# A Mamba-style decoder on one core: softplus through a PSUM bank, relu on ScalarE, and a later turn of the second half's projection

## The reference, cut to what matters

```python
ssm = x @ W_x.T                                  # 1024 -> 32 + 16 + 16
ts, Bm, Cm = (rms(ssm[..., :R]), rms(ssm[..., R:R + N]), rms(ssm[..., R + N:]))
dt = jax.nn.softplus(ts @ W_dt.T + b_dt)         # one step size for each channel and time
A = -jnp.exp(A_log)
def step(state, inp):
    dA = jnp.exp(dt_t[..., None] * A)
    state = state * dA + (dt_t * u_t)[..., None] * B_t[:, None, :]
    y = jnp.einsum('bdn,bn->bd', state, C_t)
```

## Time and profile before

| | |
|---|---|
| median of 3 runs | 1512.21 us (1509.62 to 1515.13) |
| the profiled execution | 1510.68 us, its span 1508.8 us |
| mean granted TensorE clock | 0.953 |
| the loop's scans | first starts at 132.45 us; rounds 32, 64 and 96 start at 248.90, 365.33 and 483.70 us |
| a loop round without softplus work | 2.68 us |

### The profile page before, as it was taken

How to read it: one execution, slowest core, us unless ns; L and a number is a source line. 1 busy time by engine, 2 the same in 40 slices (tenths; PEclk the granted TensorE clock), 3 DMA queues, 4 the chain that set the end, 5 groups by cost and what they waited for, 6 DMA issues and landing times.

```text
span 1508.8 us, 18407 instructions
## 1 busy us (share of the span) xinstructions
PE 1332.5 (88%) x6448; PEld 959.5 (64%) x6448; DVE 967.0 (64%) x1687; ACT 741.5 (49%) x1447; POOL 670.0 (44%) x488
## 2 busy tenths in 40 slices
PE   7996767768768988988999999799999899999996
PEld 5884556556557665444455555478888788778774
DVE  6745978978878987688654443554444456455566
ACT  4446779779778884122122222254444344434431
POOL 3228769769769871121461111263333244333321
PEclk9998889879979999999999999699999999999999
DMA  4121000013000005100200000132212122111110
GB/s 142 43 113 57 1 0 1 1 56 112 1 1 1 1 1 163 70 15 1 90 2 27 15 1 15 42 107 68 66 68 70 56 84 71 63 63 60 53 57 28
DMA packets 29546, 71.20 MB, mean 47 GB/s; under 512 B 3376, under 2 KB 3632, under 8 KB 27536
## 3 DMA queue, kind: packets, MB, share of 16 engines
q1 hardware_dynamic: 29456, 70.04, 13.9%
HBM read 67.86 MB, written 2.16 MB: 46 GB/s over the span
## 4 chain that ended last, share of the span: by engine, by line
PE 66%; DVE 15%; ACT 9%; issue 6%; POOL 2%; DMA 1%; SPq 0%; DVEq 0%; POOLq 0%; ACTq 0%
PE psum L453 9%; PE psum L455 9%; PE psum L454 9%; ACT arena L889 6%; DVE arena L1550 5%; PE psum L524 5%; PE psum L837 4%; PE psum L707 3%; PE psum L864 3%; PE psum L701 3%; PE psum L538 3%; ACT psum L889 2%; PE psum L618 2%; PE psum L549 2%; PE psum L856 2%
## 5 line engine op out<-in xcount | busy, mean ns | idle before, releaser
L1550 DVE TENSOR_TENSOR_SCAN arena<-psum,arena 128x512 f32<-128x512 f32 x256 | 298.0, 1208 | 74.2 <-ACT psum L889 74.1
L1296 POOL TENSOR_TENSOR arena<-arena 128x1024 f32<-128x1024 f32 x128 | 302.1, 2381 | 88.0 <-DVE arena L1550 86.7
L1229 POOL TENSOR_TENSOR w_split<-arena,w_split 128x512 fp32r<-128x512 f32 x128 | 168.1, 1334 | 311.9 <-ACT w_split L889 311.8
L524 PE MATMUL psum<-prm,arena 128*128 128x128 f32 x1024 | 179.3, 308 | 106.2 <-DVE arena L1550 66.6
L524 PEld LDWEIGHTS psum<-prm,arena 128*128 128x128 f32 x1024 | 127.0, 155 | 177.4 <-DVE arena L1550 128.2
L889 ACT ACTIVATE arena<-psum,ssmn 128x256 f32<-128x256 f32 x480 | 191.7, 497 | 51.5 <-PE psum L524 50.5
L889 ACT ACTIVATE arena<-psum 128x512 f32<-128x512 f32 (+2 forms) x178 | 100.8, 577 | 232.8 <-PE psum L707 53.6
L889 ACT ACTIVATE psum<-arena,amat 128x508 f32<-128x508 f32 x256 | 172.2, 725 | 30.9 <-DVE arena L1550 30.7
L889 ACT ACTIVATE arena<-arena 128x512 f32<-128x512 f32 x112 | 69.5, 633 | 228.0 <-DVE arena L1765 223.7
L538 PE MATMUL psum<-prm,arena 128*128 128x128 f32 x1024 | 148.5, 293 | 0.1
L889 ACT ACTIVATE arena<-psum,prm 128x512 f32<-128x512 f32 (+1 forms) x130 | 89.4, 700 | 117.5 <-PE psum L701 54.3
(11 more groups left out here) (221 smaller groups left out, 2475.7 us busy)
## 6 DMA issues: line engine op xcount, KB each, us to landing
arena<-wq SPq DMA_DIRECT2D x64, 256.0 KB, 2.5
arena<-wo SPq DMA_DIRECT2D x64, 256.0 KB, 2.9
arena<-bc_scratch SPq DMA_DIRECT2D x8, 1024.0 KB, 4.8
arena<-win SPq DMA_DIRECT2D x16, 256.0 KB, 2.6
arena<-xT SPq DMA_DIRECT2D x8, 256.0 KB, 6.1
x_tok<-xtok SPq DMA_DIRECT2D x1, 2048.0 KB, 8.1
arena<-wout SPq DMA_DIRECT2D x8, 256.0 KB, 5.5
arena<-ctxtok SPq DMA_DIRECT2D x1, 2048.0 KB, 8.0
```

Source lines behind the costliest of these rows:

```text
L524: last = nc.tensor.transpose(hT[:, c, b % 2, e, :], hst[:, (2 * k + e) % 4, b * L:(b + 1) * L], ident)
L1229: gp.tensor_tensor(out_, whole, hi.bitcast(F32), ALU.subtract).then_inc(done, 1)
L1296: gp.tensor_tensor(bu[:, i % 4, :, :], dtu[:, (2 * j + e) % 4, :].unsqueeze(1).to_broadcast([P, NG, HT]), Brep[:, q * NG:(q + 1) * NG, :], ...
L1550: v.tensor_tensor_scan(hst[:, i % 4, :], dA[:, i % 3, :], bu[:, (k // NG * 2 + e) % 4, k % NG, :], 0.0, ALU.mult, ALU.add).then_inc(S.scan ...
```

## The change

Four things are edited. (1) `dt_bank` gives the first four blocks banks of their own (6, 7, 5, 3); `dt_proj` no longer waits for a relu, and from block 4 on waits until the previous block's correction is done (`dt_w`), since the bank is now in use until then. (2) e is written into the block's PSUM bank in place of the tile dt in SBUF, and both instructions of `one_plus` read it there. (3) Relu is computed on ScalarE, right ahead of |v|, and is gone from VectorE. (4) `ssm_turn(1)` moves from ahead of `in_proj(31)` to round 22 of the loop and its evacuation `turned_ssm(1)` to round 23; on GpSimd `ssm_rstd(1)` moves ahead of `step_size(1)` and `step_in(1)`.

```diff
+        def dt_bank(M):
+            return bank[(6, 7, 5, 3)[M] if M < GP else 5]
...
             def dt_proj(M):
                 h, m = M // MD, M % MD
-                if M % MD in (0, GP):
-                    pe.wait_ge(S.ssmT_sb, (1 if M == 0 else 2))
+                if m == 0:
+                    pe.wait_ge(S.ssmT_sb, h + 1)
                 if M >= GP:
-                    pe.wait_ge(S.dt_relu, M)
-                elif M >= 2:
-                    pe.wait_ge(S.dt_relu, M - 1)
-                mm(bank[6 + M % 2 if M < GP else 5][:, :], wdt_sb[:, m * P:(m + 1) * P], ssmT[0:RK, h, :],
+                    pe.wait_ge(S.dt_w, M)
+                mm(dt_bank(M)[:, :], wdt_sb[:, m * P:(m + 1) * P], ssmT[0:RK, h, :],
...
-            in_proj(BACK + 4)
-            in_proj(BACK + 5)
-            ssm_turn(1)
-            in_proj(BACK + 6)
-            pe.wait_ge(S.dt_relu, GP)
+            for n in range(BACK + 4, len(UNITS)):
+                in_proj(n)
+            pe.wait_ge(S.dt_w, GP)
...
+                if k == 22:
+                    pe.wait_ge(S.dt_w, 2 * GP)
+                    ssm_turn(1)
...
             def abs_dt(M):
                 act.wait_ge(S.dt_proj, M + 1)
-                av(dt[:, M % MD, :], bank[6 + M % 2 if M < GP else 5][:, :], ACT.Abs,
-                   bias=pc("bdt")[:, M % MD:M % MD + 1]).then_inc(S.dt_abs, 1)
+                bias = pc("bdt")[:, M % MD:M % MD + 1]
+                av(sp_r[:, M % GP, :], dt_bank(M)[:, :], ACT.Relu, bias=bias).then_inc(S.dt_relu, 1)
+                av(dt[:, M % MD, :], dt_bank(M)[:, :], ACT.Abs, bias=bias).then_inc(S.dt_abs, 1)
 
             def exp_dt(M):
                 act.wait_ge(S.dt_abs, M + 1)
-                av(dt[:, M % MD, :], dt[:, M % MD, :], ACT.Exp, scale=-1.0).then_inc(S.dt_exp, 1)
+                av(dt_bank(M)[:, :], dt[:, M % MD, :], ACT.Exp, scale=-1.0).then_inc(S.dt_exp, 1)
...
-            in_out(BACK + 4)
-            in_out(BACK + 5)
-            turned_ssm(1)
-            in_out(BACK + 6)
+            for n in range(BACK + 4, len(UNITS)):
+                in_out(n)
...
+                    if k == 23:
+                        turned_ssm(1)
...
-            for M in range(2):
-                step_size(M)
-                step_in(M)
+            step_size(0)
+            step_in(0)
             ssm_rstd(1)
+            step_size(1)
+            step_in(1)
...
-            def relu_dt(M):
...
             def one_plus(M):
                 dve.wait_ge(S.dt_exp, M + 1)
-                v.tensor_scalar(sp_w[:, M % GP, :], dt[:, M % MD, :], 1.0, None, ALU.add).then_inc(S.dt_w0, 1)
+                v.tensor_scalar(sp_w[:, M % GP, :], dt_bank(M)[:, :], 1.0, None, ALU.add).then_inc(S.dt_w0, 1)
                 dve.wait_ge(S.dt_w0, M + 1)
-                v.scalar_tensor_tensor(out=dt[:, M % MD, :], in0=sp_w[:, M % GP, :], scalar=1.0, in1=dt[:, M % MD, :],
+                v.scalar_tensor_tensor(out=dt[:, M % MD, :], in0=sp_w[:, M % GP, :], scalar=1.0, in1=dt_bank(M)[:, :],
                                        op0=ALU.subtract, op1=ALU.subtract).then_inc(S.dt_w, 1)
...
-                    if r in (4, 8, 12, 16):
-                        relu_dt(M + r // 4 - 1)
```

More of the change, by code:

```diff
@@ L1519, in ssm_normed @@
                         ins.then_inc(S.ssm_norm, 1)
-            def relu_dt(M):
-                dve.wait_ge(S.dt_abs, M + 1)
-                v.tensor_scalar(sp_r[:, M % GP, :], bank[6 + M % 2 if M < GP else 5][:, :],
-                                pc("bdt")[:, M % MD:M % MD + 1], 0.0, ALU.add, ALU.max).then_inc(S.dt_relu, 1)
             def one_plus(M):
                 dve.wait_ge(S.dt_exp, M + 1)
-                v.tensor_scalar(sp_w[:, M % GP, :], dt[:, M % MD, :], 1.0, None, ALU.add).then_inc(S.dt_w0, 1)
+                v.tensor_scalar(sp_w[:, M % GP, :], dt_bank(M)[:, :], 1.0, None, ALU.add).then_inc(S.dt_w0, 1)
                 dve.wait_ge(S.dt_w0, M + 1)
-                v.scalar_tensor_tensor(out=dt[:, M % MD, :], in0=sp_w[:, M % GP, :], scalar=1.0, in1=dt[:, M % MD, :],
+                v.scalar_tensor_tensor(out=dt[:, M % MD, :], in0=sp_w[:, M % GP, :], scalar=1.0, in1=dt_bank(M)[:, :],
                                        op0=ALU.subtract, op1=ALU.subtract).then_inc(S.dt_w, 1)
@@ L1559, in _ @@
             for M in range(GP):
-                relu_dt(M)
-            for M in range(GP):
                 one_plus(M)
```

## The result

The kernel after took 1473.93 us in the median of four runs (1470.52 to 1478.39) against 1510.91 of the kernel before: a ratio of 0.9752, with a 95% interval of 0.9718 to 0.9786. The forecast was 1480 with a range of 1466 to 1493. Measured a second time (E9), on another chip, the same kernel took 1477.15 us (ratio 0.9777, 0.9753 to 0.9802). The profiled execution took 1475.01 us; its span is 35.6 us shorter than that of before.

What follows compares the result with a forecast made beforehand. ScalarE was taken to bound plain rounds at 2.68 us, idling 4.02 us per `one_plus`. Loop 26.5 plus start 6.5 less 0.7 for the turn gave 32.3 us off 1510.68, 1478.4; forecast 1480, range 1466 to 1493.

Steps and rivals of the forecast that it cites:

- The bound and the stall: Scan loop: ScalarE bounds plain rounds at 2.68 us and idles 4.02 us (2.85 plus 1.17) for each `one_plus`.
- Why `one_plus` was slow: VectorE in the loop: its two instructions spread to medians of 1695 and 2716 ns; those with a PSUM operand don't spread.
- `one_plus` at 1.43: VectorE in the loop: with operands in PSUM, 0.73 plus 0.70 makes 1.43 us in place of 4.37.
- Idle time of ScalarE for each `one_plus`: Scan loop: falls from 4.02 to 1.05 us, saving 3.0 us for each of nine `one_plus`.
- Relu 0.57 on ScalarE: Ahead of the next decays: relu adds 0.57 us to the path for each of twelve blocks.
- e into PSUM, 0.09 more: ScalarE's exp in the loop: writing PSUM instead of SBUF costs 0.09 us more each, between 0 and 0.15.
- A cycle at 13.3 us, 2.34 less: Four loop rounds: 3.0 - 0.57 - 0.09 = 2.34 us saved, from 15.68 to 13.3; nine such cycles give 21.1.
- stretches at 1.2 GHz, which I had as a gain that might come: Warmer-TensorE rival in the loop: shorter stalls may keep 2.4 GHz, 9 us more at most, 1471 to 1477; chance 0.10.
- The start, 6.5: Ahead of the loop: without the turn the first scan starts 6.5 us earlier, limited by GpSimd's tile; bounds 4 and 7.6.
- The wait of `dt_proj`: TensorE in round 5: waiting for the correction costs 0, at most the matmul's own 0.6 us.
- GpSimd's rival: Scan loop: GpSimd, busy 12.89 us a cycle, takes over the wait; 12 us lost, 1492; chance 0.13.
- The slow `one_plus` as a rival: Scan loop: any SBUF operand holds VectorE up while GpSimd runs; loop loses 9.5 us, time 1517; chance 0.04.

Runs made afterwards that it cites:

- E9: The kernel after, unchanged, timed again beside the kernel before on another chip: 1477.15 us, ratio 0.9777.
- E1: The kernel after with e written in place into the SBUF tile dt again and read there by `one_plus`, relu still on ScalarE: 1517.09 us, ratio 1.0044.
- E3: The kernel after with e of blocks 4 to 15 in an SBUF tile of its own in place of the PSUM bank: 1516.99 us, ratio 1.0043.
- E8: The kernel before with only the second half's turn moved to round 22, its evacuation to 23 and GpSimd's power up by two: 1504.47 us, ratio 0.9965.
- E2: The kernel after with the second half's turn, its evacuation and GpSimd's power back ahead of the loop: 1478.51 us, ratio 0.9792.

## Why the prediction was right, step by step

- *The bound and the stall*: right. E1 and E3 bring the stall back (2.41 and 1.17 us, 3.6 in all for 4.02), and E8, which has the slow `one_plus` of before, keeps the cycles of before (15.67 to 16.24 us).
- *Why `one_plus` was slow*: the prediction gave no mechanism, only that instructions with a PSUM operand don't spread. The end of GpSimd's tile as what releases it was found in the traces afterwards (E3).
- *`one_plus` at 1.43*: 1.30 from start to start. L1529 was expected at 0.73 like L1523 and took 0.66; L1531 0.69 for 0.70.
- *Idle time of ScalarE for each `one_plus`*: expected 1.05, measured 0.4 to 0.5, since `one_plus` was shorter by 0.13 and TensorE's turn took 0.5 of the 0.65 I gave it; the rest of the difference I can't name. In the first cycle of a window 0.6 to 0.7 are left (E2).
- *Relu 0.57 on ScalarE*: measured 0.57. *e into PSUM, 0.09 more*: not so. It takes 0.52 from start to start (290.95 to 291.47), as from SBUF to SBUF. The decay was a poor row for it, and the Trainium skill's line on ScalarE's writes to PSUM (PSUM — Partial Sum Buffer, Specifications (TRN2)) is not contradicted; a gain from it isn't shown either.
- *A cycle at 13.3 us, 2.34 less*: the first one is 13.26, undisturbed. The other two are 12.79 and 12.91, 3.4 and 3.0 less. Here the sum was short: I had relu's leaving VectorE give something back at r = 4 only, but at r = 12 VectorE weighs as well, and that round went from 3.68 to 3.04. That, the idle time above and the 0.09 are the mis-sized terms. r = 17 to 21 gave 2.1 for 1.8. The undisturbed sum is 11 us for a window in place of 8.8; the measured windows gave 8.9, 8.8 and 10.2, since stretches at 1.2 GHz, which I had as a gain that might come, and the first round took some 4 us of it back. The stretches became fewer in windows 1 and 2 (mean clock 0.94 and 0.95; 0.88 before in window 1), not in window 0 (0.87). That the total came out so near the forecast is partly luck: the terms were short by about 2 us a window, and what I hadn't counted took most of that back.
- *The start, 6.5*: right. E8 gives 5.5 for the move with its cost in round 23, where I had 5.8. First scan expected at 125.5, measured at 126.57 with everything 1.9 late, and at 124.61 with nothing late (E9); 7.8 less the 1.2 of the longer first round is 6.6. GpSimd's tile was its limit, as I had it.
- *The wait of `dt_proj`*: 0 as expected; `one_plus` releases it 3 times for 0.5 us in all. With the slow `one_plus` of E1 it would not have been 0.
- *GpSimd's rival*: it didn't come. It stood still for 2.3 to 3.0 us in each of four cycles, waiting for a scan.
- *The slow `one_plus` as a rival*: its reason, that any SBUF operand is held up, is not borne out, since L1531 still reads one operand in SBUF and takes 0.69. It put 9.5 us on the loop, and E1's windows lost 8.1 together; but E1 has neither e nor its reads in PSUM, and waits at `dt_proj`, so the terms are not confirmed by that.
- The sum, 32.3 us, was measured as 35.7 between the two profiled executions and 37.0 between the medians. Of the difference some 2 us lie in the loop and 1.7 us behind it, in code that didn't change; the rest is the spread of the medians.

## What to carry to other kernels

When the same instruction takes 0.69 us in one place and 2.72 in another, look at what GpSimd does beside it before looking at the instruction, and lay the ends side by side: one operand moved to PSUM made it fast again, and was worth 40 to 43 us against the same kernel with that operand in SBUF. Ask where the freed engine now waits, and whether a share of the new bound's work fits into that wait: that, with the plain rounds' share taken away, gave another 14 to 17 us, of which all weighings on ScalarE alone had given 5 to 9. Work shared out at even distances is worth checking round by round, since in rounds where the sharing engine has no slack it costs more than it saves.

## What the runs showed of the hardware that I had not expected

- VectorE adding a constant to 128x512 float32 from PSUM took 0.66 us, and with a bias operand and a maximum 0.73.
- A two-operand SBUF instruction of VectorE beside a GpSimd tile ended 0.55 us after the tile did, in each of 36 cases. The slow values are nearly constant (2.710 to 2.736 us in E3) as it always started at the same distance from the tile's end.
- TensorE's granted clock falls to 0.5 for stretches of a few us in the loop. There eight transposes take 1.9 us in place of 1.04, and TensorE, otherwise with slack, becomes the bound. What decides at which rounds this falls stays open: two executions of one program had it in the same rounds but for one stretch, while E2, with the same instructions and the same wait of 2.02 us there, did not have it in those.
